# Feature-crossing tower: the first tile's products before the weight additions, other load and copy orders

## The reference, cut to what matters

```python
e  = stack([tbl_f[ids[:, f]] for f in range(26)], axis=1)      # 512 x 26 x 32, gathered rows
x1 = einsum('bik,bjk,hij->bhk', e, e, W1) + b1[None, :, None]  # W1: 128 x 26 x 26
x2 = einsum('bik,bjk,hij->bhk', x1, e, W2) + b2[None, :, None] # W2: 128 x 128 x 26
z  = sum(concatenate([x1, x2], axis=1), axis=-1)               # 512 x 256
h  = concatenate([z, dense_ctx], axis=1)                       # 512 x 272
h  = maximum(h @ W_top1 + b_top1, 0)                           # 512 wide
h  = maximum(h @ W_top2 + b_top2, 0)                           # 256 wide
y  = h @ W_top3                                                # 512 x 1
```

## Time and profile before

| what | value |
|---|---|
| median of three executions | 182.67 us |
| the profiled execution, its own time | 182.35 us |
| its span from first to last instruction | 180.6 us |
| TensorE busy | 159.1 us, 88% of the span |
| VectorE busy | 122.6 us, 68% |
| ScalarE busy | 79.0 us, 44% |
| GpSimd busy | 69.7 us, 39% |
| bytes moved by DMA | 9.43 MB |

### The profile page before, as it was taken

How to read it: one execution, slowest core, us unless ns; L and a number is a source line. 1 busy time by engine, 2 the same in 40 slices (tenths; PEclk the granted TensorE clock), 3 DMA queues, 4 the chain that set the end, 5 groups by cost and what they waited for, 6 DMA issues and landing times.

```text
span 180.6 us, 3364 instructions
## 1 busy us (share of the span) xinstructions
PE 159.1 (88%) x1277; PEld 149.1 (83%) x1277; DVE 122.6 (68%) x371; ACT 79.0 (44%) x204; POOL 69.7 (39%) x72
## 2 busy tenths in 40 slices
PE   6599999342599999996999999979997999999995
PEld 6599999342599988995899898969986999899993
DVE  5534779999996578999449969964848994242000
ACT  2154445079446530087435715554345426554022
POOL 2606147566585445365544644664460000000000
PEclk9879999999579999999999999999999999999999
DMA  5999613000000000400000000000000000000000
GB/s 182 401 370 362 228 28 137 7 11 9 11 6 11 4 15 6 154 11 11 7 7 15 9 7 16 11 7 7 11 14 1 4 0 2 4 0 0 4 0 0
DMA packets 4802, 9.43 MB, mean 52 GB/s; under 512 B 1553, under 2 KB 3089, under 8 KB 4786
## 3 DMA queue, kind: packets, MB, share of 16 engines
q1 hardware_dynamic: 2130, 6.42, 9.9%
q0 software_dynamic: 2048, 1.05, 3.3%
q10 hardware_dynamic: 608, 1.74, 2.6%
HBM read 9.21 MB, written 0.00 MB: 51 GB/s over the span
## 4 chain that ended last, share of the span: by engine, by line
PE 75%; DVE 10%; ACT 7%; issue 3%; DMA 3%; SPq 0%; DVEq 0%
PE bank L349 17%; PE bank L362 12%; PE bank L357 10%; PE bank L294 9%; PE bank L310 6%; DVE folded L690 5%; PE bank L397 4%; PE bank L368 4%; ACT diag L518 3%; DMA w1p<-in_w1p_dram 3%; PE bank L387 2%; PE bank L385 2%; PE bank L390 2%; PE bank L374 2%; DVE prod L644 1%
## 5 line engine op out<-in xcount | busy, mean ns | idle before, releaser
L266 POOL DMA_INDIRECT rows<-in_tbl_dram,idx x64 | 68.8, 1075 | 64.3 <-DMA rows<-in_tbl_dram,idx 48.3
L349 PE MATMUL bank<-diag,prod 128*128 128x108 f32 x256 | 33.7, 287 | 8.8 <-ACT diag L518 5.3
L349 PEld LDWEIGHTS bank<-diag,prod 128*128 128x128 f32 x256 | 31.8, 200 | 10.6 <-issue 7.5
L679 DVE COPY t<-bank 13x128 f32<-13x128 f32 (+1 forms) x64 | 16.8, 263 | 24.7 <-PE bank L357 24.0
L518 ACT ACTIVATE diag<-prod,quad 128x416 f32<-128x416 f32 (+2 forms) x48 | 22.1, 544 | 16.3 <-DVE prod L644 16.3
L362 PEld LDWEIGHTS bank<-t,v 128*128 128x128 f32 x208 | 24.8, 192 | 1.8 <-issue 0.4
L498 ACT COPY t<-bank 128x432 f32<-128x432 f32 x32 | 15.0, 521 | 24.1 <-PE bank L349 24.1
L362 PE MATMUL bank<-t,v 128*128 128x128 f32 x208 | 25.2, 276 | 0.3 <-ACT v L477 0.3
L294 PE MATMUL bank<-small,idb 128*128 128x256 f32 (+1 forms) x80 | 23.6, 413 | 1.7 <-DVE w1p L628 1.7
L628 DVE TENSOR_TENSOR w1p<-bank,chosen 128x320 f32<-128x320 f32 (+2 forms) x32 | 17.0, 533 | 9.7 <-PE bank L294 7.3
L357 PE MATMUL bank<-diag,prod 128*77 128x64 f32 x256 | 20.8, 235 | 0.0
(11 more groups left out here) (68 smaller groups left out, 176.3 us busy)
## 6 DMA issues: line engine op xcount, KB each, us to landing
idb<-in_idt_dram SPq DMA_DIRECT2D x4, 640.0 KB, 8.7
wt<-in_W_top_dram SPq DMA_DIRECT2D x2, 512.0 KB
rows<-in_tbl_dram,idx POOLq DMA_INDIRECT x64
w2t<-in_w2t_dram ACTq DMA_DIRECT2D x1, 768.0 KB, 9.3
small<-in_small_dram SPq DMA_DIRECT2D x1, 768.0 KB
small<-in_small_dram SPq DMA_DIRECT2D x1, 672.0 KB, 10.6
w1t<-in_w1t_dram SPq DMA_DIRECT2D x1, 640.0 KB, 15.0
w1p<-in_w1p_dram SPq DMA_DIRECT2D x1, 521.0 KB, 5.4
```

Source lines behind the costliest of these rows:

```text
L266: pool.indirect_dma_start(rows[t][:, f, :], None, tables[f], bass.IndirectOffsetOnAxis(ap=idx[:, t, f:f + 1], axis=0)).then_inc(s_got[t][p ...
L349: mm = nc.tensor.matmul(m0[:, g % GBANK, :, 0:JW], prod[:, G, 0:P], diag[:, G, :, :], start=True, stop=True)
L679: ins = nc.vector.tensor_copy(t1[p0:p0 + HALF, GRAM + slot:GRAM + slot + nb, n], m1[64:64 + HALF, :].rearrange("p (n j) -> p j n", n=NSTEP ...
```

## The change

It has these parts:

- **Order on TensorE, tile 0.** The steps of tile 0 come right after the ctB pieces. The v0 and v1 pieces all come behind them: upper v0, v1, the first 13 fields of z2, lower v0, `z2_low` (the former `z2_last`), then the rest of z2 with the look-ups of tile 1 between its pieces. v0 and v1 pieces no longer use bank 7. Before the upper v0 pieces TensorE waits until all four steps have been copied out.
- **Fillers.** 16, 8 and 6 filler matmuls, the 8 behind the turn of part 1, the 6 behind that of part 2.
- **Order on VectorE, tile 0.** Turn of part 0, first half of the low additions, `products_a`, turn of part 1, second half of the low additions, `one_hot(1)`, `products_b`, and only then `cross_a` and `cross_b`.
- **Copies.** ScalarE makes the factor copies of parts 0 and 1 and the wrap copy, in all tiles; VectorE keeps that of part 2. There are two factor banks (6 and 7), so a factor copy waits for all picks of its tile. In tile 0 ScalarE also makes the four `bands` copies of each step.
- **Loads.** w1p goes from SP to the head of ScalarE's queue, ahead of w2t. idt 1 comes earlier; w1t and the top weights wait on SP until the 13 folds have been taken.
- **Later tiles.** `layer3` writes bank 6, so step 1 has no wait for `copy_y`. One look-up goes behind each of steps 0 and 1. Picks 4 and 5 come ahead of the turn of part 0, and the turn of part 1 ahead of `half_a`. ScalarE's `spread(t+1, 2)` comes ahead of `relu1(t)`; in tile 0 the factor copies of tile 1 and `spread(1, 1)` come behind `relu1(0)` and `spread(1, 2)` behind `relu2(0)`.
- The lines of the gathers and their pauses are not touched.

```diff
-LOOKED = [(), (0, 1), (2, 3), (4, 5)]
+LOOKED = [(0,), (1,), (2, 3), (4, 5)]
-FILL = 16
+FILLS = [16, 8, 6]
-HOME = [RING[q % len(RING)] for q in range(DONE["ctB"])] + [0, 1, 2, 0] + [3, 4, 5, 7] + [0, 1, 2, 0]
+HOME = [RING[q % len(RING)] for q in range(DONE["ctB"])] + [0, 1, 2, 0] + [3, 4, 5, 3] + [4, 5, 0, 3]
-BEHIND = {8: 0, 9: 1, 11: 2, 12: 3, FOLDS: 4, FOLDS + 1: 5, FOLDS + 2: 6, FOLDS + 3: 7}
+BEHIND = {5: 0, 6: 1, 8: 2, 9: 3, 10: 4, 11: 5, 12: 6, 13: 7}
-        L2, L3 = bank[1:3], bank[3]
-        factor = bank[6][:, 0:GROUPS * HALF].rearrange("p (g f) -> p g f", f=HALF)
+        L2, L3 = bank[1:3], bank[6]
+        factors = [bank[6 + i][:, 0:GROUPS * HALF].rearrange("p (g f) -> p g f", f=HALF) for i in range(2)]
...
             sp.dma_start(idx[:], io["ids"]).then_inc(s_idx, 16)
-            sp.dma_start(w1p[:], io["w1p"]).then_inc(s_w1p, 16)
...
+            sp.dma_start(idb[:, 1, :], on_all(io["idt"], 1)).then_inc(s_idb[1], 16)
+            sp.wait_ge(s_sf, FOLDS)
+            sp.dma_start(w1t[:], io["w1t"]).then_inc(s_w1t, 16)
             sp.dma_start(wt1[:], ...)
             sp.dma_start(wt1c[:], ...)
             sp.dma_start(wt2[:], ...)
-            sp.dma_start(w1t[:], io["w1t"]).then_inc(s_w1t, 16)
-            sp.dma_start(idb[:, 1, :], on_all(io["idt"], 1)).then_inc(s_idb[1], 16)
...
-                if t and pick == 1:
+                if t and pick == 0:
                     pe.wait_ge(s_pb, t * PRODS)
+                if t > 1 and pick == 1:
+                    pe.wait_ge(s_y, t - 1)
...
-                if s == 1:
-                    if t:
-                        pe.wait_ge(s_y, t)
-                    else:
-                        pe.wait_ge(s_sf, DONE["v1"])
+                    if t == 0:
+                        pe.wait_ge(s_sf, DONE["ctB"])
...
+            for i, n in enumerate(FILLS):
+                if i:
+                    pe.wait_ge(s_turn[i], 1)
+                for _ in range(n):
+                    nc.tensor.matmul(bank[0][:, 0:P], ident[:], ident[:], start=True, stop=True)
+            for s in range(STEPS):
+                step(0, s)
+            pe.wait_ge(s_e0, STEPS)
+            pe.wait_ge(s_e1, STEPS)
+            pe.wait_ge(s_eg, STEPS)
             for q in range(DONE["ctB"], DONE["v1"]):
                 make(q)
             pe.wait_ge(s_sf, HIGH)
+            z2(0, HALF)
+            for q in range(DONE["v1"], len(SETUP)):
+                make(q)
+            pe.wait_ge(s_sf, DONE["v1"])
+            z2_low(0, False)
+            look_up(1, 0)
+            look_up(1, 1)
+            pe.wait_ge(s_sf, len(SETUP))
+            for i, (j0, j1) in enumerate(((13, 17), (17, 22), (22, FIELDS))):
+                z2(j0, j1, j1 == FIELDS)
+                look_up(1, 2 + 2 * i)
+                look_up(1, 3 + 2 * i)
...
         @block.scalar
+            act.dma_start(w1p[:], io["w1p"]).then_inc(s_w1p, 16)
...
+                    if t == 0:
+                        for dst, src in bands(s):
+                            ins = nc.scalar.copy(dst, src)
+                        ins.then_inc(s_eg, 1)
...
+            def take_factor(t, part):
+                f0, f1, col, _ = PARTS[part]
+                act.wait_ge(s_turn[part], t + 1)
+                act.wait_ge(s_pick, (t + 1) * len(PICKS))
+                nc.scalar.copy(factors[part][:, :, 0:f1 - f0], prod[:, :, col:col + f1 - f0]).then_inc(s_fac[part], 1)
+                if part == 1:
+                    nc.scalar.copy(prod[:, :, COL_B + HALF:COL_B + HALF + WRAP],
+                                   prod[:, :, COL_B:COL_B + WRAP]).then_inc(s_dup, 1)
...
+            for q in range(FOLDS + 1):
+                take(q)
+            take_factor(0, 0)
+            for q in range(FOLDS + 1, FOLDS + 5):
                 take(q)
             spread(0, 0)
+            for q in range(FOLDS + 5, DONE["ctB"]):
                 take(q)
+            take_factor(0, 1)
             spread(0, 1)
+            spread(0, 2)
+            evict(0)
+            for q in range(DONE["ctB"], len(SETUP)):
                 take(q)
+            act.wait_ge(s_vec, 32)
             for t in range(TILES):
+                more = t < TILES - 1
+                if t:
+                    evict(t)
+                    if more:
+                        spread(t + 1, 0)
+                        take_factor(t + 1, 0)
+                        take_factor(t + 1, 1)
+                        spread(t + 1, 1)
...
                 if t == 0:
                     spread(1, 0)
+                elif more:
+                    spread(t + 1, 2)
                 relu1(t)
                 if t == 0:
+                    take_factor(1, 0)
+                    take_factor(1, 1)
                     spread(1, 1)
                 relu2(t)
+                if t == 0:
+                    spread(1, 2)
...
         @block.vector
             def half_a(t):
-                turn(t, 1)
-                take_factor(t, 0)
-                dve.wait_ge(s_fac, t * len(PARTS) + 1)
-                products_a(nc.vector, prod, factor).then_inc(s_pa, 1)
+                dve.wait_ge(s_fac[0], t + 1)
+                products_a(nc.vector, prod, factors[0]).then_inc(s_pa, 1)
...
+            turn(0, 0)
+            dve.wait_ge(s_sf, FOLDS)
             low = low_terms(folded)
             add(low, 0, False)
+            half_a(0)
+            turn(0, 1)
             add(low, 1, True)
+            one_hot(1)
+            half_b(0)
             dve.wait_ge(s_sf, DONE["ctA"])
             (cross_a, then cross_b)
...
             for i in range(len(PICKS)):
                 pick(1, i)
-                if i == 3:
+                if i == 5:
                     turn(1, 0)
+            turn(1, 1)
             half_a(1)
             half_b(1)
```

More of the change, by code:

```diff
@@ L212, in dlrm_tower @@
         s_dup = sem("s_dup")
-        s_fac = sem("s_fac")
+        s_fac = [sem(f"s_fac{i}") for i in range(3)]
         s_pa = sem("s_pa")
@@ L231, in dlrm_tower, with bands @@
         s_out = sem("s_out")
+        def bands(s):
+            m1 = bank[3 * (s % 2) + 2]
+            n = slice(s * NSTEP, (s + 1) * NSTEP)
+            return [(t1[p0:p0 + HALF, GRAM + slot:GRAM + slot + nb, n],
+                     m1[64:64 + HALF, :].rearrange("p (n j) -> p j n", n=NSTEP)[:, HALF - JLOW + b:HALF - JLOW + b + nb])
+                    for p0, b, nb, slot in BANDS]
         block = ctx.enter_context(nc.Block())
@@ L322, in make @@
                 elif kind == "v1":
-                    if HOME[q] >= 6:
-                        pe.wait_ge(s_pick, len(PICKS))
                     for i in range(n):
@@ L358, in step, with z2, z2_low @@
                 mm.then_inc(s_m1, 1)
-            def z2(j0, j1):
+            def z2(j0, j1, end=False):
                 for j in range(j0, j1):
-                    nc.tensor.matmul(Z2[:, 0:P], v0[:, J2[j], :], t0[:, J2[j], :], start=j == 0, stop=False)
-            def z2_last(t):
+                    mm = nc.tensor.matmul(Z2[:, 0:P], v0[:, J2[j], :], t0[:, J2[j], :], start=j == 0,
+                                          stop=end and j == j1 - 1)
+                if end:
+                    mm.then_inc(s_z2, 1)
+            def z2_low(t, end):
                 pe.wait_ge(s_e1, (t + 1) * STEPS)
@@ L367, in z2_last @@
                     k = slice(0, C1 if x == GRAM - 1 else 64 + C1)
-                    mm = nc.tensor.matmul(Z2[:, 0:P], v1[k, x, :], t1[k, x, :], start=False, stop=x == GRAM - 1)
-                mm.then_inc(s_z2, 1)
+                    mm = nc.tensor.matmul(Z2[:, 0:P], v1[k, x, :], t1[k, x, :], start=False, stop=end and x == GRAM - 1)
+                if end:
+                    mm.then_inc(s_z2, 1)
             def z1():
@@ L412, in _ @@
             pe.wait_ge(s_sf, FREE[DONE["ctB"]])
-            for _ in range(FILL):
-                nc.tensor.matmul(bank[0][:, 0:P], ident[:], ident[:], start=True, stop=True)
+            for i, n in enumerate(FILLS):
[8 more added lines that the diff above has]
+            pe.wait_ge(s_eg, STEPS)
             for q in range(DONE["ctB"], DONE["v1"]):
@@ L417, in _ @@
             pe.wait_ge(s_sf, HIGH)
-            pe.wait_ge(s_pad, 1)
-            for t in range(TILES):
+            z2(0, HALF)
[10 more added lines that the diff above has]
+                look_up(1, 3 + 2 * i)
+            pe.wait_ge(s_pad, 1)
+            pe.wait_ge(s_z1w, 1)
+            pe.wait_ge(s_vec, 32)
+            pe.wait_ge(s_wt, 48)
+            z1()
+            layer1(0)
+            layer2(0)
+            for t in range(1, TILES):
                 more = t < TILES - 1
@@ L667, in half_b @@
                 dve.wait_ge(s_dup, t + 1)
-                dve.wait_ge(s_fac, (t + 1) * len(PARTS))
+                dve.wait_ge(s_turn[2], t + 1)
+                nc.vector.tensor_copy(factors[1][:, :, f0 - HALF:f1 - HALF], prod[:, :, col:col + f1 - f0]).then_inc(s_fac[2], 1)
+                dve.wait_ge(s_fac[2], t + 1)
                 for s in range(PRODS):
```

(18 more changed lines are left out.)

65 lines of the change are left out of this document (9 added, 56 removed).

## The result

The changed kernel takes 182.69 us (median of 20 executions) where the kernel before takes 181.58 us (20 executions): ratio 1.009, 95% interval 1.0058 to 1.0122. So it is about 1% slower, less than the 2% that would count as a change. The forecast was 183.5, with a change of +1.2 us on the traced execution; measured are 182.69 and, between the two medians, +1.1 us.

What follows compares the result with a forecast made beforehand. TensorE's work plus its stands and slow stretches were taken to bound the kernel. Terms -6.1 - 2.3 + 6.0 + 3.4 + 2.3 - 2.1 = +1.2 on the profiled 182.35 us gave 183.5 us, 80% range 179.0 to 187.5.

Steps and rivals of the forecast that it cites:

- Start of tile 0: Ahead of tile 0's steps: gathers and VectorE end together, so step 0 starts at 41.2 us instead of 47.3, -6.1.
- late weights meet the gathers: Rival at tile 0's bursts 3 and 4: late loads slow them by 1.8 and up to 3.2 us; 187.0 us, chance 0.18.
- The early loads bring the gathers forward: Front of tile 0: with w1t and top weights moved away, the second burst lands at 19.0 us, 2.7 earlier.
- Clock in the steps: Tile 0's steps: fillers leave a longest stand of about 1.7 us, so less low clock; about -2.3 us.
- Steps' end to z1: Tile 0 behind its steps: waits for copies, transposes in the open and takes make 14.6 us into 20.6, +6.0.
- Handover: Tile 0 to 1: products_a waits for a factor copy behind relu1, +3.4 us; low clock in the first step, +2.3.
- Later tiles: Tiles after the handover: step 1's wait for y goes and look-ups wait less for picks; -2.1 us.
- relu1 behind a spread: Rival in tiles 1 and 2: spread(t+1, 2) delays relu1(t), 1.5 us each give 186.5 us; chance 0.10.

Runs made afterwards that it cites:

- first yardstick: The changed kernel as it is, run again beside the kernel before on one chip: 182.71 us against 180.35, ratio 1.0173.
- shown by the fillers: Changed kernel with 16 filler matmuls behind layer 2 of tile 0, in the stand before tile 1: 180.56 us, ratio 1.0046 to the kernel before.
- the kernel in which the stand is gone: Changed kernel with all look-ups of tile 1 earlier and ScalarE's tile 1 copies ahead of the z2 copy: 172.83 us, 0.9493 of the kernel before.
- the last kernel of the list: Changed kernel with early look-ups, late loads behind the turn of part 2, tile 0's copies ahead of waits for tile 1's gathers: 170.25 us, 0.9379 of kernel before.

## Why the prediction was right, and where it was off

- **Start of tile 0.** Right to 0.9 us (42.08 for 41.2), by errors that partly offset. The second burst landed at 19.1 as forecast (19.0), the third landed after 3.4 us (3.5 forecast). The fourth took 4.51 instead of 2.1, as the loads of 2.3 MB still ran (121 GB/s between its last issue and its landing); the last burst of four took 4.9 us to issue instead of 5.2. So the turn of part 1 came at 36.32 instead of 34.9 us, and VectorE stood 4.33 us for it; from there to the turn of part 2 (40.24) it needed 3.9 us where the forecast had 4.5. The rival "late weights meet the gathers" thus had the right place and 2.3 of its 5.0 us; the run with the loads behind the bursts puts what they cost at 3.5 us of start.

```profile
36.32 0.72 DVE L685 STREAM_TRANSPOSE prod<-rows 128x320 f32<-128x320 f32 x1 [4.33 <-DMA rows<-in_tbl_dram,idx]
```

- **The early loads bring the gathers forward** was the step that failed in substance: the second burst did land 2.7 us earlier, but with the loads back at the front the start is at 42.44, so at most 0.4 of the 5.2 us come from moving them. The other 4.9 come from the rest of the change. That this is mainly the order on VectorE, which lets the gathers bind in place of the additions, is argued from the traces; no run takes these parts singly.
- **Clock in the steps.** -2.4 for -2.3; the run without the later fillers gives 13.7 to 13.9 us for the steps, so the fillers are the cause. The longest stand between them was not the forecast 1.7 us but 2.7 (34.42 to 37.09), and the clock held.
- **Steps' end to z1.** +7.4 for +6.0. The terms of work were right: 2.16 us of stand (2.2), and 20.6 us in the traces in which the clock holds, exactly the sum. Missed was that the clock can fall in a stand of 2.2 us. I took the earlier trace rows, where 1.8 us left it at 1.00, as the rule, and overlooked that the same trace of before has a stand of 2.0 us at its start (5.36 to 7.40) with half clock behind it:

```profile
6.00:7.00 1.00, 0.00 (x0) 0.00 (x0) 0.41 (x2) 0.00 (x0) 0.69 (x2) 1.00 1.06 415
...
8.00:9.00 1.00, 1.00 (x5) 1.00 (x5) 0.00 (x0) 0.41 (x1) 0.16 (x1) 0.50 1.04 372
```

- **Handover.** +3.0 for +3.4 and +1.6 for +2.3. The low clock ended within the first step in this trace; in the first yardstick it lasted over the whole step, 5.8 us. Mechanism and order are shown by the fillers, by the factor copy ahead of relu1, and by the kernel in which the stand is gone.
- **Later tiles.** -4.3 for -2.1 between the traces. In the trace of before TensorE waits there for y (1.0 us), for picks (1.7 us, 1.5 of it at once) and at a late start of tile 2 (0.65 us), 3.3 us in all, of which I had counted 2.1; in the changed kernel's trace none of these waits is left. The remaining 1.0 us stays open. Whether other executions of the kernel before have the long pick wait and the late start no trace shows. Its median over 20 executions is 181.58 us, 0.8 below the traced one, while the changed kernel's traced execution lies 0.3 below its median of 182.69. That is how two equal traces and a ratio of 1.009 go together.
- **relu1 behind a spread** did not bite: in tile 1 the last spread ended at 116.5 and relu1 could start at 117.4, 0.9 us later.

```profile
115.19 1.28 ACT L539 ACTIVATE diag<-prod,quad 128x96 f32<-128x96 f32 x4
...
117.43 0.37 ACT L556 ACTIVATE h<-bank,vec 128x128 f32<-128x128 f32 x1 [0.95 <-issue]
```

That the whole came out within 1 us of the forecast is in part luck. By stretches the forecast missed by +0.9, -0.1, +1.4, -0.4, -0.7 and -2.2 us: the later start and the missed fall of the clock offset the overrated handover and later tiles. Together that made +0.1 between the traces for the +1.2 forecast, and the +1.1 between the medians comes with it only because the traced execution of before was slower than its median. The mechanism (an earlier start, paid back behind the steps and in the handover) is as forecast. Open is what decides in which executions the clock falls in the stand of 2.16 us.

## What to carry to other kernels

When work is pulled ahead of a stall that used to hide other work, list what the stall hid, and find a new cover for it in the same edit: here two look-ups in the first stand, the picks of the next tile in the 11.65 us in which VectorE waited for its first look-up, and ScalarE's copies for the next tile moved ahead turned a loss of 1% into a gain of 5%. At a handover between tiles, look at each engine's queue for what stands ahead of the next tile's first producer, and keep the current tile's copies ahead of whatever waits for a transfer. Delaying loads helps only if nothing waits for the transfers beside which they then run: behind the folds they slowed bursts on the path and brought nothing, behind all bursts of tile 0 they slowed only a burst that had time to spare and brought 3.6 to 5 us, and once tile 1 had been pulled forward that same burst had no time to spare any more.

## What the runs showed of the hardware

- The granted clock fell in a TensorE stand of 2.16 us in some executions of the same program and not in others: 0.65 over the 4.91 us behind it in the changed kernel's first trace, 1.00 in the yardstick's on another chip. Of the nine traces that keep this stand unfilled (2.15 to 2.97 us) it fell in three, those of 2.16, 2.48 and 2.97 us. It also fell after 2.0 us at the start of the kernel before and after 1.88 us in the last kernel of the list. It fell each time in or right behind the stands of 4.9 us, and with 3.7 us of fillers in one of them it did not. The Trainium skill, "TensorE: Matmul & The Clock Gate", part 1, says that without activity the gate falls back to half rate. The traces behind the stands of 4.9 us agree (0.50 to 0.64 over the step behind them).
- The third and fourth burst of gathers of tile 0 (three gathers each) together took 7.2 to 8.6 us from last issue to landing in the nine traces in which the late loads went out behind the folds, and 4.2 to 4.5 us in the four (that of before among them) without a bulk load beside them. Single bursts: 1.5 to 3.0 us in most cases without a load, but 3.2 to 3.9 in a few (3.67 in the kernel before from 65.57, with 9 GB/s moving), and up to 6.36 beside the loads.
- A gather's issue on GpSimd took 0.94 us, and up to 3.07 us in the changed kernel's trace while VectorE did the cross additions:

```profile
54.44 3.07 POOL L274 DMA_INDIRECT rows<-in_tbl_dram,idx  x1 [0.30 <-issue]
```

- ScalarE's factor copy of 128x416 into PSUM took 0.52 us, VectorE's had taken 0.64.
